# Attention inside one kernel: both heads' value products in two 64-column halves of TensorE, and the softmax sums added up on VectorE and GpSimd

## What is computed

```python
att = jax.nn.softmax(jnp.einsum('bthd,bshd->bhts', q, k), axis=-1)
o = jnp.einsum('bhts,bshd->bthd', att, v).reshape(B, T, D)
```

## Time and profile before

| | us |
|---|---|
| three runs | 1919.29, 1926.11, 1923.94 |
| median | 1923.94 |
| the profiled execution | 1924.25 |
| its span in the trace | 1922.5 |
| attention stage in the trace | 476 to 1641 |

### The profile page before, as it was taken

How to read it: one execution, slowest core, us unless ns; L and a number is a source line. 1 busy time by engine, 2 the same in 40 slices (tenths; PEclk the granted TensorE clock), 3 DMA queues, 4 the chain that set the end, 5 groups by cost and what they waited for, 6 DMA issues and landing times.

```text
span 1922.5 us, 31032 instructions
## 1 busy us (share of the span) xinstructions
PE 1782.2 (93%) x10495; PEld 1606.7 (84%) x10495; DVE 1193.4 (62%) x2345; ACT 723.1 (38%) x1346; POOL 356.6 (19%) x355
## 2 busy tenths in 40 slices
PE   2999988876999999999999999989999999899998
PEld 1788656746899999998989889889999999697996
DVE  7678678874656556654765746665656665774332
ACT  1223211034755445445455544354545544120110
POOL 3213101003213011020100003100000012564440
PEclk9999999977999999999999999999999999999999
DMA  3101000011031000030000000000000002111111
GB/s 111 34 7 45 12 12 25 9 60 39 6 124 44 28 12 7 1 124 12 12 12 12 6 1 18 23 12 12 6 12 7 6 1 76 44 60 44 44 33 54
DMA packets 24782, 58.00 MB, mean 30 GB/s; under 512 B 2537, under 2 KB 4805, under 8 KB 24013
## 3 DMA queue, kind: packets, MB, share of 16 engines
q1 hardware_dynamic: 24650, 56.18, 9.0%
HBM read 44.87 MB, written 11.30 MB: 29 GB/s over the span
## 4 chain that ended last, share of the span: by engine, by line
PE 83%; DVE 8%; issue 3%; DMA 2%; DVEq 2%; ACT 1%; POOL 1%; SPq 0%; POOLq 0%; ACTq 0%
PE ps L2320 22%; PE ps L2205 13%; PE ps L2375 7%; PE ps L2263 6%; PE ps L2302 6%; PE ps L2306 6%; PE ps L1991 5%; PE ps L2404 4%; PE ps L2128 3%; PE ps L2004 2%; PE ps L2331 1%; DMA tok_a<-in_x 1%; DVE share L1759 1%; DVE onehot L1582 1%; DVE max_part L1742 1%
## 5 line engine op out<-in xcount | busy, mean ns | idle before, releaser
L2320 PE MATMUL ps<-p_raw,v_ones 125*128 125x250 f32 x2080 | 529.1, 376 | 9.7 <-DVE feat L1761 6.2
L1742 DVE TENSOR_REDUCE max_part<-ps 125x2 f32<-125x500 f32 x520 | 330.4, 675 | 215.5 <-PE ps L2263 204.9
L1316 ACT ACTIVATE p_raw<-ps 125x500 f32<-125x500 f32 x520 | 304.4, 587 | 333.7 <-PE ps L2306 329.1
L2320 PEld LDWEIGHTS ps<-p_raw,v_ones 125*128 125x128 f32 x2080 | 362.1, 191 | 36.7 <-issue 7.7
L1759 DVE RECIPROCAL share<-ps 64x250 f32<-64x250 f32 x120 | 206.3, 1719 | 86.1 <-PE ps L2320 83.5
L2302 PE MATMUL ps<-q_both_a,k_both_a 128*125 128x250 f32 x520 | 184.2, 374 | 1.8 <-issue 1.8
L2302 PE MATMUL ps<-q_both_b,k_both_b 128*125 128x250 f32 x520 | 182.5, 372 | 0.0
L909 POOL CAST w_hi<-w_raw 128x512 fp32r<-128x512 f32 x44 | 28.3, 644 | 811.2 <-issue 353.2
L1582 DVE TENSOR_SCALAR onehot<-iota_h,win_key,key_t 125x320 f16 x453 | 177.0, 391 | 0.3 <-issue 0.3
L2205 PE MATMUL ps<-xa_hi,w_hi 128*128 128x418 f32 (+1 forms) x448 | 150.3, 335 | 13.3 <-POOL w_lo L911 9.1
L1581 DVE TENSOR_SCALAR onehot<-iota_h,low_t 125x125 f16 x453 | 128.7, 284 | 48.2 <-issue 28.1
(11 more groups left out here) (390 smaller groups left out, 3440.3 us busy)
## 6 DMA issues: line engine op xcount, KB each, us to landing
w_raw<-in_w_mlp SPq DMA_DIRECT2D x32, 256.0 KB, 2.7
w_raw<-in_w_gps SPq DMA_DIRECT2D x16, 256.0 KB, 2.6
w_raw<-in_w_tp SPq DMA_DIRECT2D x16, 256.0 KB, 2.6
w_raw<-in_w_sp SPq DMA_DIRECT2D x12, 256.0 KB, 2.6
w_raw<-in_w_cr SPq DMA_DIRECT2D x12, 256.0 KB, 2.6
d_xt<-xb_hi SPq DMA_DIRECT2D x1, 2508.0 KB, 9.3
d_xt<-xb_lo SPq DMA_DIRECT2D x1, 2508.0 KB, 14.9
xa_hi<-d_xt SPq DMA_DIRECT2D x1, 2508.0 KB, 9.9
```

The source lines that it names most:

```text
L1316: act.activation(p_raw[:, g % PR, :], ps[0:TOK, g % 2, 0:4 * TOK], ACT.Exp, scale=SCALE).then_inc(s_exp, 1)
L1742: dve.tensor_reduce(part[:, y, :, j], ps[0:TOK, bank, 0:4 * TOK].rearrange("p (h k) -> p h k", h=2), AX.X, ALU.max)\
L2320: ins = pe.matmul(ps[:, bank, 0:2 * TOK], v_ones[:, n % 2, kt, h:h + 2, :], p_raw[:, g % PR, cols], start=(b == 0 and x == 0), stop=last)
```

## The change

The order of steps becomes (n, i, b, h): the two heads of a block follow each other. `product` is issued once for both heads, at the step of head 1. Its stationary operand is 64 columns of values of one head; head 0 writes partitions 0 to 63 of the bank, head 1 partitions 64 to 127. The ones leave the product. Instead GpSimd (head 0) and VectorE (head 1) add the exponentials of a unit's blocks into `p_sum`, then its two key tiles into one, and `denominator` multiplies that by 64 columns of ones, both heads side by side, into columns 250 to 499 of the same bank. `unit_out` works once for both heads on 128 partitions. A ring of six `p_raw` tiles replaces three, and ScalarE waits for the additions as well before it reuses one.

```diff
-PR = 3
+PR = 6
-STEP = [(n, i, h, b) for n in range(PASSES) for i in range(5) for h in range(2) for b in range(blocks_in(n, i))]
+STEP = [(n, i, b, h) for n in range(PASSES) for i in range(5) for b in range(blocks_in(n, i)) for h in range(2)]
...
+ADDED = [(n, i, b) for n in range(PASSES) for i in range(5) for b in range(1, blocks_in(n, i) + 1)]
+ADD_NO = {at: x + 1 for x, at in enumerate(ADDED)}
...
@@ tensor_steps
-            steps += SIDE[g] + [("P", g)]
+            steps += SIDE[g]
+            n, i, b, h = STEP[g]
+            if h == 1:
+                steps.append(("P", g))
+                if b == 0 and g - 1 > first:
+                    steps.append(("D", 5 * n + i - 1))
+        steps.append(("D", 5 * STEP[end - 1][0] + 4))
...
-        v_ones = sb("v_ones", [TOK, 2, NT, 3, 64], F32)
+        v_rows = sb("v_rows", [TOK, 2, NT, 2, 64], F32)
+        ones_f = sb("ones_f", [TOK, 64], F32)
+        p_sum = sb("p_sum", [TOK, 2, 4 * TOK], F32)
...
@@ GpSimd, called at each step of head 0 ahead of the step's other work
+            def add_first_head(g):
+
+                n, i, b, _ = STEP[g]
+                blocks = blocks_in(n, i)
+                pool.wait_ge(s_exp, g + 1)
+                if b == min(1, blocks - 1):
+                    pool.wait_ge(s_den, 5 * n + i)
+                if b > 0:
+                    if ADD_NO[n, i, b] > 1:
+                        pool.wait_ge(s_add_a, ADD_NO[n, i, b] - 1)
+                    before = p_raw[:, (g - 2) % PR, :] if b == 1 else p_sum[:, 0, :]
+                    pool.tensor_tensor(p_sum[:, 0, :], before, p_raw[:, g % PR, :], ALU.add).then_inc(s_add_a, 1)
+                if b == blocks - 1:
+                    if ADD_NO[n, i, blocks] > 1:
+                        pool.wait_ge(s_add_a, ADD_NO[n, i, blocks] - 1)
+                    total = p_raw[:, g % PR, :] if b == 0 else p_sum[:, 0, :]
+                    pool.tensor_tensor(p_sum[:, 0, 0:2 * TOK], total[:, 0:2 * TOK], total[:, 2 * TOK:4 * TOK], ALU.add).then_inc(s_add_a, 1)
...
@@ ScalarE, exponent
                 if g >= PR:
-                    act.wait_ge(s_pv, g - PR + 1)
+                    n, i, b, h = STEP[g - PR]
+                    act.wait_ge(s_pv, (g - PR) // 2 + 1)
+                    act.wait_ge((s_add_a, s_add_b)[h], ADD_NO[n, i, max(b, 1)])
...
@@ VectorE: add_second_head is the same for head 1, on s_add_b and p_sum[:, 1, :],
@@ called at each step of head 1, ahead of the maxima
+            def unit_out(u):
+
+                out = feat[:, u // 5 % 4, 2 * TOK * (u % 5):2 * TOK * (u % 5 + 1)]
+                dve.wait_ge(s_den, u + 1)
+                dve.reciprocal(out, ps[:, 2 + u % 2, 2 * TOK:4 * TOK]).then_inc(s_share, 1)
                 dve.wait_ge(s_share, u + 1)
+                dve.tensor_tensor(out, ps[:, 2 + u % 2, 0:2 * TOK], out, ALU.mult).then_inc(s_o, 1)
...
-                    if g > first and ends(g - 1):
-                        unit_out(g - 1)
+                    if g in OUT_AT:
+                        unit_out(OUT_AT[g])
...
@@ TensorE
+            HALF = [slice(0, 64), slice(64, 128)]
...
                 for x in range(2):
                     kt, cols, last = 2 * b + x, slice(2 * TOK * x, 2 * TOK * (x + 1)), b == blocks_in(n, i) - 1 and x == 1
-                    ins = pe.matmul(ps[:, bank, 0:2 * TOK], v_ones[:, n % 2, kt, h:h + 2, :], p_raw[:, g % PR, cols], start=(b == 0 and x == 0), stop=last)
+                    for h, r in enumerate(HALF):
+                        ins = pe.matmul(ps[r, bank, 0:2 * TOK], v_rows[:, n % 2, kt, h, :], p_raw[:, (g - 1 + h) % PR, cols],
+                                        start=(b == 0 and x == 0), stop=last)
                 ins.then_inc(s_pv, 1)
+
+            def denominator(u):
+
+                n, i = u // 5, u % 5
+                bank = 2 + u % 2
+                pe.wait_ge(s_add_a, ADD_NO[n, i, blocks_in(n, i)])
+                pe.wait_ge(s_add_b, ADD_NO[n, i, blocks_in(n, i)])
+                for h, r in enumerate(HALF):
+                    ins = pe.matmul(ps[r, bank, 2 * TOK:4 * TOK], ones_f[:, :], p_sum[:, h, 0:2 * TOK], start=True, stop=True)
+                ins.then_inc(s_den, 1)
```

More of the change, by code:

```diff
@@ L58 @@
 EDGE_KEYS, EDGE_INSIDE, EDGE_BOUNDS, EDGE_DONE = 9, 21, 25, 28
-ROW = 64
 TB = [(0, 4), (4, 4), (8, 2)]
@@ L148 @@
 FIRST[PASSES, 0] = len(STEP)
-LAST = {(n, i): STEP_NO[n, i, 1, blocks_in(n, i) - 1] for n in range(PASSES) for i in range(5)}
+LAST = {(n, i): STEP_NO[n, i, blocks_in(n, i) - 1, 1] for n in range(PASSES) for i in range(5)}
+ADDED = [(n, i, b) for n in range(PASSES) for i in range(5) for b in range(1, blocks_in(n, i) + 1)]
+ADD_NO = {at: x + 1 for x, at in enumerate(ADDED)}
 def maxima(n, i):
@@ L159, in uses @@
     t0, nt = TB[b]
-    return [STEP_NO[n, i, h, x] for i in range(5) for h in range(2) for x in range(blocks_in(n, i)) if t0 <= 2 * x + 1 and 2 * x < t0 + nt]
+    return [STEP_NO[n, i, x, h] for i in range(5) for h in range(2) for x in range(blocks_in(n, i)) if t0 <= 2 * x + 1 and 2 * x < t0 + nt]
 def value_turns(n):
@@ L288, in pool_plan @@
     folded = AT["F", FB] + 8
[L289 removed]
+    for n, start in ((0, folded), (1, folded), (2, FIRST[3, 1]), (3, FIRST[4, 2]), (4, FIRST[7, 0] + 2), (5, FIRST[7, 0] + 2), (6, FIRST[7, 1]),
                      (8, FIRST[11, 0] + 4), (9, FIRST[11, 0] + 4), (10, FIRST[11, 2])):
@@ L463, in build @@
         ln_stats = sb("ln_stats", [TOK, NT, 6], F32)
-        ln_mv = sb("ln_mv", [TOK, NT, 2], F32)
+        ln_mv = sb("ln_mv", [TOK, NT, 2], F32, place["end"] + 896)
         ln_r = sb("ln_r", [TOK, 4, 2, NT], F32)
@@ L1752, in maximum, with add_second_head @@
                         .then_inc(s_max_col, 1)
[L1754 to L1759, removed]
+            def add_second_head(g):
+                n, i, b, _ = STEP[g]
+                blocks = blocks_in(n, i)
+                dve.wait_ge(s_exp, g + 1)
+                if b == min(1, blocks - 1):
+                    dve.wait_ge(s_den, 5 * n + i)
+                if b > 0:
+                    if ADD_NO[n, i, b] > 1:
+                        dve.wait_ge(s_add_b, ADD_NO[n, i, b] - 1)
+                    before = p_raw[:, (g - 2) % PR, :] if b == 1 else p_sum[:, 1, :]
+                    dve.tensor_tensor(p_sum[:, 1, :], before, p_raw[:, g % PR, :], ALU.add).then_inc(s_add_b, 1)
+                if b == blocks - 1:
+                    if ADD_NO[n, i, blocks] > 1:
+                        dve.wait_ge(s_add_b, ADD_NO[n, i, blocks] - 1)
+                    total = p_raw[:, g % PR, :] if b == 0 else p_sum[:, 1, :]
+                    dve.tensor_tensor(p_sum[:, 1, 0:2 * TOK], total[:, 0:2 * TOK], total[:, 2 * TOK:4 * TOK], ALU.add).then_inc(s_add_b, 1)
+            def unit_out(u):
+                out = feat[:, u // 5 % 4, 2 * TOK * (u % 5):2 * TOK * (u % 5 + 1)]
+                dve.wait_ge(s_den, u + 1)
+                dve.reciprocal(out, ps[:, 2 + u % 2, 2 * TOK:4 * TOK]).then_inc(s_share, 1)
                 dve.wait_ge(s_share, u + 1)
-                dve.tensor_tensor(feat[own, n % 4, 2 * TOK * i:2 * TOK * (i + 1)], ps[own, 2 + u % 2, 0:2 * TOK], share[own, :],
-                                  ALU.mult).then_inc(s_o, 1)
+                dve.tensor_tensor(out, ps[:, 2 + u % 2, 0:2 * TOK], out, ALU.mult).then_inc(s_o, 1)
             def project(j, cols, done):
@@ L1789, in last_out @@
                     fold_bias()
-            def ends(g):
-                n, i, _, b = STEP[g]
-                return b == blocks_in(n, i) - 1
+            OUT_AT = {LAST[n, i] + 3: 5 * n + i for n in range(PASSES) for i in range(5) if (n, i) not in ((7, 4), (11, 4))}
             for first, end in ((0, FIRST[8, 0]), (FIRST[8, 0], len(STEP))):
@@ L1842, in _ @@
                     last_out(task)
-                unit_out(end - 1)
+                unit_out(unit_of(end - 1))
             for p in range(3):
@@ L2355, in _ @@
                     product(*at)
+                if what == "D":
+                    denominator(*at)
                 if what == "J" and at[0] == 0:
```

47 lines of the change are left out of this document (24 added, 23 removed).

## The result

| | before | changed kernel |
|---|---|---|
| median, us (range) | 1922.23 (1919.29 to 1926.11) | 1907.05 (1906.68 to 1908.76) |
| runs | 4 | 4 |
| span of the profiled run, us | 1922.5 | 1905.4 |

The ratio is 0.9915, 95% interval 0.9899 to 0.9931: 15 us faster, where 74 were forecast. The sign and the mechanism of the gain are as predicted, the size is not.

A forecast was written before the change was run, and what follows sets the result against it. The prediction took TensorE's matmuls to bound the attention stage. From 1924.25 us: -113 products, +26 sums by ones, +15 new order, +3 stretch ends, -5 banks, giving 1850 us; own range 1815 to 1885, 8-in-10 range 1765 to 1945.

The forecast's parts named there:

- What bounds the kernel: Attention stage: as long as TensorE's matmuls, 1136 of 1165 us busy, so each microsecond taken from TensorE shortens it.
- The products: Value-probability products on TensorE: overlapping halves cut a group from 1.70 to 1.27 us, 113 us saved over 260 pairs.
- The order assumed within the halves: Within a product group: records start in order, a half's second waits for its first; eight records need 5 slots, 1.07 us.
- the switch: Around each product group: changing TensorE's array to 64-column width and back costs 0.2 us per visit, 260 times.
- The denominators: Sums by ones on TensorE: two more calls for each of 60 units, 0.43 us each, 26 us in all.
- The additions: Summing exponentials, VectorE 159 us and GpSimd 296 us more: hidden in both engines' idle time, cost nothing.
- The new order: Products wait for a later exponential: 63 of 260 pairs lack side work to cover 0.36 us, 15 us in all.
- Banks and ends: TensorE's waits for output banks mostly go, -5 us; longer ends of the two stretches of steps cost +3 us.
- Better overlap: Rival on the products: each half takes records independently, 4 slots per group; 1780 us, chance 0.20.
- No overlap: Rival on the products: halves take turns, nothing saved, switching costs 52 us and ones 51; 2040 us, chance 0.17.
- VectorE takes over: Rival on the additions: GpSimd slows VectorE's sums to 1.8 us, delaying TensorE through maxima banks and denominators; 1915 us, chance 0.12.

The follow-up runs named there:

- e4: Changed kernel with all of head 0's records of a product group issued before head 1's, instead of alternating; 1909.5 us, ratio 0.9917.
- e8: e1 with full-width products of 128 columns, which takes the overlap of the halves away and gives wrong sums; 1999.8 us, ratio 1.0388.
- e2: Changed kernel without head 1's additions on VectorE, its sums set to a constant; 1852.4 us, ratio 0.9627.
- e3: Changed kernel without head 0's additions on GpSimd, its sums set to a constant; 1890.4 us, ratio 0.9825.
- e1: Changed kernel with the maxima put ahead of head 1's addition in VectorE's list of each step; 1873.0 us, ratio 0.9732.
- e10: e1 with GpSimd's additions of the residual held until the last denominator is computed; 1863.4 us, ratio 0.9691.
- e5: e1 with two blocks' products in one group of 16 records, for about half the mode switches; 1899.0 us, ratio 0.9863.

## Why the prediction was right in sign and wrong in size

**What bounds the kernel: right for before, not for after.** TensorE's work is what the change took away, and taking it away alone didn't shorten the stage as much, because TensorE now waits.

**The products: right mechanism, two sizes off.** Predicted 5 slots and 0.2 us of switch, 1.27 us and 113 us in all; measured 4 slots and 0.33 us, 1.18 us and 135 us. The order assumed within the halves was wrong (e4); the switch costs more than any row that I leaned on. "TensorEngine Tiling (Array Packing)" of the Trainium skill (Key Properties) has both rules, and the runs agree with both: tiles that work independently, and a price for a change of mode, which the page calls a drain, here 0.33 us. e8 confirms the sum, with the waits that it gave back.

**The denominators: right.** 0.42 us for a call pair's four records behind a group (1.42 us against 1.00), 25 us over 60 units; predicted 26.

**The additions: the step that failed.** "The idle time of both engines hides all of it: cost nothing." Head 1's cost 55 us (e2), and head 0's 17 us (e3). The amounts were near: GpSimd 307 us for 296, VectorE 206 for 159. VectorE was idle for a third of the stage, as I wrote. But an engine works in order, and what counts is what stands ahead of the result that TensorE wants next. In every second step an addition of 0.7 to 1.7 us was set ahead of the maxima, and once per unit it stood right behind a reciprocal of 1.7 us. I asked of GpSimd what its additions stand in line with; of VectorE I compared only totals. e1 moves the additions behind the maxima: 34 of the 55 us come back. e2 against e1 leaves 21, of which 6.8 stand at the end of the stage: from the last product to the output projection it is 7.7 us in e2 and 14.5 in e1. e10 gets 6.6 us at the same place by moving the residual's additions away from the last sums. The rest is not told apart.

**The new order: better than feared.** Predicted 63 waits of the product for an exponential and 15 us; measured 24 and 7.3. A TensorE that waits elsewhere lets the exponentials catch up, which fits e1: with fewer other waits it has 29 and 9.0.

**Banks and ends.** The banks' wait of 6.2 us became 2.0 (predicted: -5). The end of the stage was put at +3 for two ends; the last one alone is +9.7 us (4.8 to 14.5), and still +3.1 once GpSimd is held (7.9, e10), with 1.9 us of the residual's tiles still between the last sums on VectorE. At the first end TensorE waits 4.2 us for GpSimd's last sum, which stands behind weight splits; the term had the additions' own length alone.

**The sum in these terms.** Products -135, denominators +25. Waits that the views name: L2319, L2308, L2250, L2366 and L2377 stand for 89 us in the changed kernel, their counterparts of before for 29: +60, with 8.4 of the last end in it. Half-clock stretches in the stage grew from 27 to 68 us, which is at most +20 when all of it is work. Together -30, measured -17 in the profiled spans. At least 13 us are in no term of mine, and more if the half clock cost less than 20.

**The rivals.** Better overlap was true as a mechanism, and its number, 1780, still wrong, for the same step as mine failed. No overlap is excluded. "VectorE takes over", at 1915, came nearest in time. Its path was half right. VectorE working in order does hold TensorE back, but the banks of the maxima (9.1 us) and the denominators (12.6 us) are the smaller part; the largest wait, 38.0 us, is that of the turned rows for the maxima themselves, which the rival didn't name. Its condition was wrong: sums of 1.8 us and an engine full. VectorE is only 66% busy, its sums take 0.8 to 1.0 us on average, and it is late nevertheless. The low chance came from testing it as a question of load.

**Open.** The forecast and e2 agree partly by luck: my products were 22 us too dear, my waits 8 us too many, and e2 still has 20.5 us of turned rows that I didn't foresee, and more half-clock time than the kernel before (114 against 108 us). Whether the additional half-clock time is a cause or a consequence of the waits was not tested by itself; it falls along with them (161 us in the changed kernel, 152 in e1, whose profiled execution was the slowest of its four, 123 in e10, 114 in e2).

## What to carry to other kernels

When work moves to an engine with idle time, don't ask whether it fits, ask what it stands in front of: write down that engine's list around the result that the bounding engine wants next, and put the new work behind it. Two lines in another place were worth 34 us here, more than twice what the whole change had given. And check which engine's work runs beside the last, uncovered piece of a stage.

## What the runs showed of the hardware

- Two 64-column halves start their matmuls in pairs, 6 to 7 ns apart, or 13 ns where one half's four records were issued ahead of the other's (e4): eight 250-column records of 32-bit data in four slots of 0.21 us.
- A visit to the 64-column mode costs 0.33 us. The 0.15 us of it that lie within the group are the same for 8 and for 16 records (e5). Behind the group the first full-width weight load starts together with its matmul, not ahead of it, and that matmul takes 0.22 us instead of 0.12.
- A 500-column sum of two SBUF tiles takes VectorE 0.68 us alone and up to 1.76 us if it starts during an instruction of GpSimd. "SBUF — State Buffer" of the Trainium skill (SBUF: two separate sides) says that one blocks the other for a whole instruction. The trace agrees: the sums held up in this way end 0.53 to 0.54 us after GpSimd's instruction, whenever they started, as the one at 1106.86 us does, which takes 1.43 us.
- When TensorE waited at the end of the stage (8.4 us, then 5.0 us), its granted clock was 0.5 for 17.1 us from 1617.2 us on, and for 10.2 us with the shorter waits of e10 (2.6 and 4.4 us).
